# A two-layer graph kernel on one core: first loads on three queues, the first batch's x in halves, two score rows wider, a split end, and new orders on every engine

## The reference, cut to what matters

```python
u = einsum('bnh,bmh->bnm', x, x) / sqrt(H)
delta = softmax(u) * adj                       # adj is 0 or 1
att = delta / (sum(delta, axis=2) + 1e-10)
# above the diagonal with Wl, on it with Ws, below it with Wr
ctx = att_left @ (x @ Wl.T + bl) + att_self @ (x @ Ws.T + bs) + att_right @ (x @ Wr.T + br)
x1 = layernorm(x + relu(ln_w * norm(ctx) + ln_b))
d = (sum(adj, -1) + 1e-5) ** -0.5
out = layernorm(x1 + (d * adj * d) @ (x1 @ W1) + b1)
```

## Time and profile before

| what | value |
|---|---|
| median of three runs | 443.6 us (442.7 to 443.77) |
| the profiled execution, its own time | 445.5 us |
| its span, first to last instruction | 443.8 us |
| TensorE busy (matmuls) | 431.7 us, 97% |
| DVE busy | 381.1 us, 86% |
| ACT busy | 318.7 us, 72% |
| POOL busy | 302.2 us, 68% |

### The profile page before, as it was taken

The page is one execution under the profiler, slowest core; times in us unless marked ns, Lnnn a source line. Parts: engine busy times, 40 slices in busy tenths (PEclk is TensorE's granted clock), DMA queues, the critical chain, the costliest instruction groups (busy, mean ns, idle before and its releaser), DMA issues. The chain is left out here.

```text
span 443.8 us, 9076 instructions
## 1 busy us (share of the span) xinstructions
PE 431.7 (97%) x2775; PEld 355.7 (80%) x2775; DVE 381.1 (86%) x699; ACT 318.7 (72%) x674; POOL 302.2 (68%) x364
## 2 busy tenths in 40 slices
PE   7999999999999999999999999999999999999984
PEld 4789989779787888869887797977987789897743
DVE  2899898997999889997999989999799988998536
ACT  2588887778677787678876787677777777887420
POOL 2034666668777778758796687766877596897882
PEclk9999999999999999999999999999999999999998
DMA  5925859489765885468943888538866589254801
GB/s 163 350 68 146 264 162 258 143 214 257 151 185 136 246 244 136 153 168 280 220 141 111 204 273 216 178 110 216 267 137 189 142 245 273 55 132 98 199 19 54
DMA packets 68880, 79.91 MB, mean 180 GB/s; under 512 B 7232, under 2 KB 60608, under 8 KB 68832
## 3 DMA queue, kind: packets, MB, share of 16 engines
q1 hardware_dynamic: 68768, 79.26, 65.3%
q0 software_dynamic: 64, 0.07, 0.1%
HBM read 38.40 MB, written 4.19 MB: 96 GB/s over the span
## 5 line engine op out<-in xcount | busy, mean ns | idle before, releaser
L1481 POOL TENSOR_TENSOR dM<-dT,parts 128x384 f32<-128x384 f32 x64 | 72.5, 1132 | 67.4 <-ACT dT L851 54.9
L517 PE MATMUL ps_c<-h_sum,dT 128*128 128x128 f32 x896 | 110.4, 275 | 0.0
L517 PEld LDWEIGHTS ps_c<-h_sum,dT 128*128 128x128 f32 x896 | 106.4, 192 | 2.9 <-issue 2.5
L537 PE MATMUL ps_y<-aT,x1p 128*128 128x512 f32 x224 | 106.3, 593 | 0.0
L838 ACT ACTIVATE d_rows<-ps_u,nmax 128x1024 f32<-128x1024 f32 x62 | 68.8, 1110 | 49.4 <-DVE nmax L1124 49.3
L1124 DVE TENSOR_REDUCE nmax<-ps_u 128x1 f32<-128x1024 f32 x62 | 75.2, 1213 | 18.9 <-PE ps_u L483 16.9
L1131 DVE CUSTOM_DVE_ANT_0 d_rows<-d_rows,a_rows 128x1024 f32<-128x1024 f32 x64 | 83.7, 1315 | 0.3
L851 ACT ACTIVATE dT<-ps_d 128x1024 f32<-128x1024 f32 x64 | 65.4, 1022 | 25.7 <-PE ps_d L502 23.4
L1138 DVE STREAM_TRANSPOSE a_blk<-a_rows 128x1024 f32<-128x1024 f32 x64 | 77.7, 1228 | 0.0
L857 ACT ACTIVATE junk<-a_rows 128x1024 fp8e4<-128x1024 f32 x64 | 67.2, 1049 | 0.3
L502 PEld LDWEIGHTS ps_d<-parts,d_rows 128*128 128x128 f32 x512 | 58.9, 140 | 10.5 <-issue 9.8
(11 more groups left out here) (104 smaller groups left out, 751.6 us busy)
## 6 DMA issues: line engine op xcount, KB each, us to landing
a_rows<-in_adj_dram SPq DMA_DIRECT2D x64, 512.0 KB, 4.6
aT<-a_blk SPq DMA_DIRECT2D x224, 128.0 KB, 3.2
x_rows<-in_x_dram SPq DMA_DIRECT2D x8, 512.0 KB, 3.9
a_rows<-a_blk SPq DMA_DIRECT2D x32, 128.0 KB, 2.4
out_dram<-fin SPq DMA_DIRECT2D x15, 256.0 KB, 2.6
x_turned<-x_blk SPq DMA_DIRECT2D x96, 32.0 KB, 1.9
out_dram<-fin SPq DMA_DIRECT2D x1, 192.0 KB, 2.1
fin<-in_L_gnn_Wl_dram SPq DMA_DIRECT2D x1, 64.0 KB, 3.6
```

Source lines behind the costliest of these rows:

```text
L517: pe.matmul(ps_c[:, c_place(b, i), :], dT[:, i % 2, j, :], h_sum[:, b % 2, j, k * H:(k + 1) * H], start=t == 0, stop=False)
L537: last = pe.matmul(y_bank(b, i0, i1), gathered(b)[:, j, :], turned(b)[:, i0:i1, :, j, :].rearrange("p i q c -> p (i q) c"), start=j == 0, ...
L1481: pool.tensor_tensor(dM[:, i % 2, :, :], dT[:, i % 2, i, :].rearrange("p (a c) -> p a c", a=1).to_broadcast([P, 3, P]), parts[:, :, :], AL ...
```

## The change

- SP now issues x of batch 0 as two halves, with a semaphore for the first. The weights are issued on ACT's queue, the three biases and the three norm constants on POOL's. adj's loads follow x at once, in a new order.
- The zero products of the start are two of 512 and 256 columns from 128 zeroed ones, and TensorE waits for two of POOL's constants instead of six. Both halves of x are turned before the weights, and scores(0, 0) and scores(0, 1) come ahead of the first projection.
- In batch 0 odd projections go to the bank `ps_y`, and a projection waits for the add_bias two before it.
- `first_column` makes rows 3 and 7 of batches 1 to 7 begin one block further left. The `keep` of row 6 and one piece of row 2's go.
- The last norm is (v - mean) * power. In the last batch, rows 0 to 6 keep the form with a shift and are done by ACT, which also stores rows 4 to 6; only for these are nmean and shift still computed. The statistics of an odd last block read that block twice rather than its neighbour and it.
- In the last batch the gathers over source blocks 4 to 7 are split at block 6, and row 7's gather stands behind those of rows 4 to 6.
- The lists of all five engines are in a new order. In `batch`, what stood at the head of a list (scores(p, 6) and (p, 7), turn_d(p, 4) and (p, 5), the second half of x_low) stands at the tail of the one before.

```diff
+        def h_bank(b, j):
+            return (ps_y if b == 0 and j % 2 else ps_m)[:, 0:3 * H]
+
         def kept_before(b, i):
-            return (NB - 1) * (b - 1) + i
+            return (NB - 2) * (b - 1) + min(i, NB - 2)
+
+        def first_column(i):
+            return i - (i % HB == HB - 1)
...
+        def scaled_by_act(b, i1):
+            return b == B - 1 and i1 < NB
...
         def norm_f_on(eng, b, i0, i1):
-            eng.wait_ge(f_scale, NB * b + i1)
+            eng.wait_ge(f_power, NB * b + i1)
             for i in range(i0, i1):
                 v = fin[:, i, :]
-                last = eng.tensor_scalar(v, v, power["f"][:, i:i + 1], shift["f"][:, i:i + 1], ALU.mult, ALU.add)
+                mean = f_stats_of(i, 1) if b == B - 1 and i >= NB - 2 else stats["f"][:, i, 1:2]
+                last = eng.tensor_scalar(v, v, mean, power["f"][:, i:i + 1], ALU.subtract, ALU.mult)
...
-                load_x(p)
-                load_weights()
-                load_biases()
+                load_x_half(p, 0)
+                load_x_half(p, 1)
                 load_a(p, 0)
-                load_a(p, 3)
                 load_a(p, 1)
-                load_a(p, 2)
-                load_a(p, 5)
-                load_a(p, 6)
                 load_x(b)
...
             def first_products():
                 pe.wait_ge(warm_in, 1)
-                for c in (slice(0, HALF), slice(HALF, HALF + 3 * P)):
-                    pe.matmul(ps_u[:, c], d_rows[:, 0, 0:P], d_rows[:, 0, 0:c.stop - c.start], start=True, stop=True)
+                zero = d_rows[:, 0, 0:P]
+                for n in (HB, 2):
+                    pe.matmul(ps_u[:, 0:n * P], zero, zero.rearrange("p (a c) -> p a c", a=1).to_broadcast([P, n, P]),
+                              start=True, stop=True)
...
-                j0 = 0 if halves(b) else i
+                j0 = 0 if halves(b) else first_column(i)
                 for c in (slice(j0 * P, HALF), slice(max(j0 * P, HALF), N)):
+                    if b == 0 and i < HB:
+                        pe.wait_ge(xt_split, 2 if c.start else 1)
...
+                if b == 0 and j % 2:
+                    pe.wait_ge(xt_split, 2)
+                    wait(pe, h_added, j - 1)
...
                 turn_x(p, 0)
+                turn_x(p, 1)
                 turn_weights()
-                turn_x(p, 1)
+                scores(p, 0)
+                scores(p, 1)
                 m_read_x(p, 0)
                 project(p, 0)
-                scores(p, 0)
-                scores(p, 1)
+                project(p, 1)
+                scores(p, 2)
...
                 gather(b, 0, HB, 0, HB)
                 gather(b, HB, NB - 1, 0, HB)
-                gather(b, NB - 1, NB, 0, 2)
-                gather(b, 0, HB, HB, NB)
+                gather(b, 0, HB, HB, NB - 2)
+                gather(b, 0, HB, NB - 2, NB)
                 gather(b, HB, NB - 1, HB, NB - 2)
+                gather(b, HB, NB - 1, NB - 2, NB - 1)
                 m_read_o(p, HB, NB)
                 second_product(b, 0, HB)
-                gather(b, HB, NB - 1, NB - 2, NB)
-                gather(b, NB - 1, NB, 2, 5)
+                gather(b, HB, NB - 1, NB - 1, NB)
+                gather(b, NB - 1, NB, 0, 2)
                 second_product(b, HB, NB - 1)
-                gather(b, NB - 1, NB, 5, NB)
+                gather(b, NB - 1, NB, 2, HB)
+                gather(b, NB - 1, NB, HB, NB - 2)
+                gather(b, NB - 1, NB, NB - 2, NB)
                 second_product(b, NB - 1, NB)
...
+            def load_weights():
+                for k, w in enumerate((Wl, Wr, Ws)):
+                    act.dma_start(wraw[:, k, :], w).then_inc(const_in, 16)
...
+            def norm_f(b, i0, i1):
+                act.wait_ge(f_scale, i1)
+                act.wait_ge(f_norm, NB * b + i0)
+                normalize(fin, fin, "f", i0, i1).then_inc(f_norm, i1 - i0)
+
+            def store(b, i0, i1):
+                act.wait_ge(f_norm, NB * b + i1)
+                act.dma_start(x_block_rows(out, b, i0 * P, i1 * P), fin[:, i0:i1, :]).then_inc(fin_free[i0 // HB], 16)
```

More of the change, by code:

```diff
@@ L387, in first_batches, with batch @@
                 load_a(b, 5)
-                load_a(b + 1, 2)
+                load_a(b + 1, 1)
                 load_a(b + 1, 0)
+                move_rows(b)
+                load_a(b + 1, 3)
+                load_a(b + 1, 4)
+            def batch(b, p):
+                load_a(b, 2)
+                move_blocks(p, 0)
+                move_blocks(p, 1)
+                store(p - 1, 0, HB)
+                load_a(b, 5)
+                load_x(b + 1)
+                load_a(b, 7)
+                load_a(b + 1, 0)
+                load_a(b, 6)
+                store(p - 1, HB, NB)
                 load_a(b + 1, 1)
@@ L951, in first_batches @@
                 exps(b, 4)
+                d_out(b, 2)
+                keep(b, 4)
+                norm_x(p, HB, NB)
                 degree(b, 2)
-                keep(b, 4)
-                d_out(b, 2)
-                degree(b, 3)
-                norm_x(p, HB, NB)
+                diagonal(b, 1)
                 d_out(b, 3)
@@ L1245, in first_batches @@
                 x_low(p, 0)
+                x_low(p, 1)
+                turn_blocks(p, 0)
                 weights()
-                x_low(p, 1)
+                row_max(p, 0)
+                row_max(p, 1)
                 add_bias(p, 0)
-                row_max(p, 0)
+                masked(p, 0)
                 add_bias(p, 1)
-                row_max(p, 1)
+                row_max(p, 2)
                 add_bias(p, 2)
-                masked(p, 0)
-                row_max(p, 2)
+                masked(p, 1)
+                masked(p, 2)
                 add_bias(p, 3)
@@ L1402, in last_batches @@
                 masked(b, 2)
+                add_bias(b, 7)
                 row_max(b, 3)
-                add_bias(b, 7)
                 turn_blocks(b, 1)
                 turn_blocks(b, 2)
+                turn_blocks(b, 3)
+                row_max(b, 4)
                 masked(b, 3)
-                row_max(b, 4)
                 stats_x(p, HB, NB)
```

600 lines of the change are left out of this document (290 added, 310 removed).

## The result

The changed kernel takes 448.2 us, median of 6 runs (447.81 to 449.03), against 443.69 for the kernel before on the same chip: ratio 1.0103, 95% interval 1.0085 to 1.0122. The forecast was 437.5 us, range 435.2 to 441.5, so the result is 10.7 us off and on the other side of "no change". The profiled execution took 449.03 us with a span of 447.2; before, 445.5 and 443.8.

A forecast was written before the change was run, and what follows sets the result against it. TensorE, busy 399.06 of 400 us in the middle, was taken as the bound; -3.0 - 1.1 - 1.1 - 1.3 + 0.4 = -6.1 us from the profiled 445.5 gave 439.4, carried to the median 437.5 us, range 435.2 to 441.5.

The forecast's parts named there:

- The last norm: All batches but the last drop nmean and shift; DVE and POOL have idle time in the middle, so nothing gained.
- The start: First batch: earlier loads and shorter zero products let scores begin at 7.0 us; -3.0 us, bounds -1.2 and -3.8.
- Rival 2: At the start, early loads hinder one another, weights land at 6.8; start gains only 1.2 us, total 439.3; 10%.
- a slow clock: First batch's matmuls at 1.2 instead of 2.4 GHz, about 1.3 to 2.0 us; 1.7 kept in the sum.
- Rows 3 and 7 wider: Scores of batches 1 to 7: wider matmuls, one transpose fewer, -0.08 us a row, -1.1 us for 14 rows.
- Rival 3: In rows 3 and 7, widening costs in proportion to columns, three times 0.05 us a row: 440 us; 2%.
- The end: Last batch: split gather fills TensorE's wait, -1.1 us; last product to last norm 2.6 instead of 3.91, -1.3.
- The new orders: Middle: handover from add_out of rows 4 to 7 to the next projection is level; +0.4 us for six batches.
- rival 1: Between batches, that add_out handover is not level, TensorE waits 0.2 to 0.9 us a batch: say 440.5 us; 16%.
- Rival 4: Between batches, last x_low waits for ACT; late DVE delays the next batch, at 3 us late 446 us; 5%.
- the best ends: Most favourable bounds for start, wider rows, last gathers and tail, said to lead down to 435.2 us.

The follow-up runs named there:

- Experiment 3: Changed kernel, old norm form: POOL's loads held for the weights, 442.79 us; adj held, 445.97; weights on SP, POOL held, row 0's turn_blocks later, 443.21.
- f3_bias_behind: Changed kernel with norm as (v + nmean) * power, biases on SP behind adj of rows 0 and 1, norm constants later on SP: 440.57 us, ratio 0.9913.
- b1_wide: Kernel before with only the wider rows 3 and 7 and their copies left out: 443.16 us, ratio 0.9983.
- b2_sub_norm: Kernel before with only the last norm as (v - mean) * power, shift still computed: 446.58 us, ratio 1.0058.
- e1_add_mult: Kernel before with the last norm as (v + nmean) * power: 443.09 us, a single time.
- e2_mult_sub: Kernel before with the last norm as v * power - mean * power: 447.98 us, a single time.
- c1_hold_pool: Changed kernel with the norm's old form, POOL's loads held until the weights have landed: 442.79 us, ratio 0.9969.
- a1_norm_back: Changed kernel with the norm back as v * power + shift, nmean and shift made for all batches: 443.57 us, ratio 0.9978.
- d1_loads_back: Changed kernel with the norm's old form, all first loads on SP as before, row 0's turn_blocks later: 444.88 us, ratio 1.0025.
- d2_bias_sp: Changed kernel with the norm's old form, row 0's turn_blocks later, first loads on SP in old order except weights on ACT's queue: 443.52 us, ratio 0.9997.
- f4_bias_muladd: Changed kernel with norm as v * power + shift, biases on SP behind adj of rows 0 and 1, norm constants later on SP: 441.58 us, ratio 0.9931.
- f1_add_norm: Changed kernel with POOL's last norm as (v + nmean) * power, nmean made for all batches, early loads kept: 442.94 us, ratio 0.9976.
- a2_weights_sp: Changed kernel with the three weight loads on SP behind x and ahead of adj: 448.72 us, ratio 1.0101.

## Why the prediction was wrong, point by point

**The last norm: the failed step.** The prediction read the diff's `mult, add` to `subtract, mult` as the removal of small operations: "Both engines have idle time in the middle, so nothing." It costed what went and put what stayed in a new form at nothing, though the trace of before had a row for the old form only. At 977 ns instead of 471, 56 norms are 28 us more POOL. POOL's idle time does hide most of that, but not where `masks`, DVE's operations with two SBUF inputs and the last rows_with_bias stand beside or behind it. Removed from the changed kernel it is worth 3.46 + 1.03 = 4.5 us. That this equals the difference in the medians is chance: the late start costs about as much as the other changes win. Two things add up in the 977: the subtraction (834 to 836 ns in the old lists) and the new lists, in which a norm with an addition takes 543 ns instead of 470 and one with multiply and add about 527 instead of 471.

**The start: forecast -3.0, measured +1.07.** The sum assumed that the weights land 3.6 to 4.4 us after their issue, since such loads had done so in the old order. Rival 2 named the mechanism, loads that hinder one another, and gave it 10%, but priced it at a weights' landing of 6.8; the trace shows 9.95, later than anything that the range allowed for. It had named weights after 7 us, and a wait of DVE for adj at turn_blocks of row 0 (2.59 us in after), as signs of being wrong. Experiment 3 shows the cause: without POOL's loads, or without adj, the weights are turned at 7.13 or 5.99. The first scores come at 10.50 instead of 7.0: 3.5 us of the 4.15 by which the first context product, at 28.95, is behind the forecast (24.4, and 0.4 for a turn of x that the new list has ahead of it). The slow matmuls that follow are no missing term: they cost 1.8, and the sum kept 1.7 for a slow clock. The other forecasts for the start held: x at 4.5, the table load behind the issues, and, once the loads are in an order that the lists can use, the stream's end: row_max at 9.70 in f3_bias_behind (forecast 9.1 to 9.8) and row 5's scores over at 24.79, against a forecast of 24.4 for that point; in the new list a turn of x, 0.4 us, stands ahead of it. That is in part luck: the scores began 1.0 us later than forecast (8.02), and none of the first matmuls was slow. "All SP loads of adj now start at about 1.8 instead of 4.27; what they issue past is nothing on SP" was true of the queue and missed the shared DMA engines. The Trainium skill's rule that the prediction cited against itself (DMA: Bandwidth & Descriptors, "Issuing engines are not separate DMA queues") was the one to follow; the trace agrees that loads issued by different engines delay one another, with 8.1 us for a load that took 4.4.

**Where the start was counted twice.** The profiled execution of before was 1.9 us above the median, and its first context product came at 27.88. Four of the experiments that have the old lists and loads (b1_wide, b2_sub_norm, e1_add_mult, e2_mult_sub) reach it at 26.46, 26.14, 25.73 and 26.75. So some 1.4 us of what the start was to win back was slowness of that one execution, and the prediction subtracted both the gain and the 1.9. Against the median of the five, 26.46, the repaired start of f3_bias_behind wins 1.7 us rather than 3. By the same measure the start of after costs 2.5 us and not 1.07 (its 28.95 is the middle one of three executions with its loads, 28.88 to 30.74); with +1.75 and +0.58 that is 4.8, for a difference of 4.5 between the medians.

**Rows 3 and 7 wider: right.** Forecast -1.1, measured -0.9 in the middle of b1_wide (0.16 us a batch, so 0.08 for each row, the forecast's own number). Rival 3, cost in proportion to the columns, is out. The rule that the prediction quotes for it from the Trainium skill (TensorE: Matmul & The Clock Gate, "Back-to-back issue gap") is given there for a matmul by itself; for a stream with weight loads the section has other distances, 81 ns at 128 columns and 131 at 512, and the rows here, 0.11 and 0.23 us, agree with neither.

**The end: right in kind, hidden by the norm.** With the norm repaired the wait before the last gathers is gone and the stretch from the last full second product's add_out to the last product shrinks from 17.70 to 16.23 us, -1.47 for a forecast of -1.1. The forecast of 2.6 us from the last product to the last norm comes out as 2.8 in c1_hold_pool (435.66 to 438.46) and 2.5 in f3_bias_behind (432.97 to 435.45). But the tail from the last product to the end of the span is 5.2 to 5.5 us instead of 6.0, a gain of 0.5 to 0.8 where 1.3 was forecast: from the last norm to the end it is 2.7 us, where the prediction kept 2.1. The store that ends the kernel is now ACT's of rows 4 to 6, 192 KB and 2.2 us from issue to landing, where it was one of 64 KB and 1.6 us.

**The new orders: +0.4 forecast.** The middle of a1_norm_back is 0.82 us shorter than that of b1_wide. With 1.47 of that from the gathers, the orders cost +0.65 there, and that is the one wait for h_sum that is left: its projection starts 2.08 us after context_far began instead of 1.48. In d1_loads_back, d2_bias_sp and f4_bias_muladd that wait is gone, the middle is 407.54 to 407.56, and the orders cost nothing. Projection's wait for h_sum is rival 1's place, and after shows it three times. It came from slower POOL and DVE operations, not from the handover as such.

**Together.** f3_bias_behind has what the prediction thought the change would be: no slow norm and loads in time. Its span is 5.6 us under the profiled one of before (start -3.1, middle -1.7, tail -0.8), where the sum said 6.1; its median is 3.5 us under that of before. The other 2.1 are the two profiled executions: that of before was 1.4 us above the median of these later runs, mostly by its slow start, and that of f3_bias_behind 0.7 below its own. Rival 4, the only slower case, is not what happened: the kernel was slower for two reasons, of which one had no place in the sum and the other too small a price. Two of the prediction's sums do not come out, without weight for the result: the best ends that it names (-3.8, -1.1, -1.4, -1.5) lead from 443.6 to 435.8 and not to 435.2, and rival 3's 440 needs the +1.4 us of the quoted rule, where its own three times 0.05 less a transpose of 0.11 would give about 439.2.

What stays open is what single load delays the third weight most: I held all six broadcast loads and W1 together, not one by one. Nor was the 1.0 us between the medians of f3_bias_behind and f4_bias_muladd, whose intervals overlap, followed up, nor why some starts have slow matmuls and others not.

## What to carry to other kernels

When a diff rewrites an arithmetic form, cost the operation that stays as well as those that go: an operation that no row of the trace shows has an unknown price, and idle time of its engine is no cover for what stands behind it in that engine's list. When loads move to more queues and earlier, ask of each which of them the kernel needs first, and put them in that order; the others then wait behind and not beside. Before a gain is forecast from one execution's waits, see how much of its distance to the median those same waits are.

## What the runs showed of the hardware

- POOL's tensor_scalar on 128 x 128 float32 values takes 468 to 471 ns in the mean with multiply and add in either order, and 834 to 836 ns with a subtraction as first or second step (old lists; in the new ones 525 to 543 and 977). On DVE the subtracting norm takes no longer than the other: 0.34 and 0.35 us.
- DVE's addition of two SBUF inputs of 128 x 512 takes 0.67 to 0.69 us in most places and 1.35 to 1.53 in the others (before, after, a1_norm_back). Which of its places are slow changes with the work on POOL.
- Six broadcast loads of 64 KB on POOL's queue, beside adj and x on SP's and the weights on ACT's, make the third weight's 64 KB land 7.8 to 9.5 us after its issue (after, a1_norm_back, f1_add_norm) where it takes 2.8 to 6.0 in the other kernels, with fewer loads beside it or the weights on SP ahead of adj, and take up to 12.0 us themselves; on SP's queue the same six take 3.1 to 8.6.
- After a wait of 4.14 us of TensorE the granted clock was 0.50 from 8 us to about 14.5, and the matmuls in that time cost 1.8 us more. The same half pace stands at a granted clock of 1.00 in a1_norm_back (eleven matmuls, 2.2 us) and f4_bias_muladd (six, 1.2 us), and is absent in f3_bias_behind, c1_hold_pool and a2_weights_sp.
- Starts with the same loads and lists differ by 2 us between executions (first context product at 25.73 to 27.88). The middle differs by less than 0.3 between executions that have the same waits (409.64 and 409.90 with the old lists; 408.14 to 408.21 with the new ones and one wait for h_sum, 407.54 to 407.56 without it).
